# Two-layer conditioned transformer: the order of work at the start of the MLPs and of the layer-1 attention

## The chip, the cores and the metric

The kernel runs on one core of one Trainium2 chip. The metric is the device time of the kernel in microseconds (us); lower is better. The clock of TensorE that the throttle granted was 0.99 of full speed over the profiled execution.

## What is computed

The input x has 128 sequences of 32 tokens with 128 features, and each sequence has a condition vector of 128. Everything is float32. Cut to what matters:

```python
# layer 0: 16 heads of 8
tp = silu(cond) @ Wt + bt                # shift, scale, gate for attention and for the MLP
h = layernorm(x, g1, be1) * (1 + scale_msa) + shift_msa
h = attention(h, Wqkv, bqkv, Wproj, bproj)      # softmax over the 32 tokens of the sequence
x = x + gate_msa * h
h = layernorm(x, g2, be2) * (1 + scale_mlp) + shift_mlp
x = x + gate_mlp * (gelu(h @ W1 + b1) @ W2 + b2)
# layer 1: one head of 128
h = film(rmsnorm(x, norm1_w), cond, film1_w, film1_b)
Q, K, V = h @ q_w + q_b, h @ k_w + k_b, h @ v_w + v_b
x = x + softmax(Q @ K.T / sqrt(128)) @ V @ proj_w + proj_b
h = film(rmsnorm(x, norm2_w), cond, film2_w, film2_b)
x = x + gelu(h @ mlp_w1 + mlp_b1) @ mlp_w2 + mlp_b2
```

## The kernel before, in words

The 4096 tokens are 32 tiles of 128 rows, handled as eight groups (NG = 8) of four tiles. The kernel has four phases: layer-0 attention (phase 0), layer-0 MLP (1), layer-1 attention (2), layer-1 MLP (3). All of x stays in the tile X. A group in a phase has the running number gg = 8 * phase + g, and buffers with two halves are indexed by p = g % 2. Each engine has its own hand-written instruction list, and the order in that list is the order of the work: there is no scheduler. The engines meet through counting semaphores. Each phase is software-pipelined: while group g is multiplied, group gg + 2 is transposed, and the statistics of group gg + 3 are taken.

The path of one group into a phase's matmuls is a chain over four engines, which the steps below speak of as the normalisation chain:

- VectorE (DVE): `row_stats` (L463), `aggregate` (L471 to L483: mv, then sqm, mk, v_sb).
- GpSimd (POOL): `power` (L319 rstd, L321 shift). In phase 2 it is `mean_square` on DVE (L583) and `power1` (L398) instead.
- ScalarE (ACT): `apply` (L750) writes xhat. In phase 2 POOL's `scale_rows` (L391) does.
- TensorE (PE): `rows_T` (L919) transposes xhat into the PSUM bank hT_ps.
- DVE: `modulate` (L492) multiplies it into hA; POOL: `add_shift` (L332) adds the shift, giving h.

In an MLP step PE runs `up(phase, g)` (L943, four chunks of 128x512, into banks 2 to 5), `rows_T(gg + 2)`, then `down(phase, g - 1)` (L1129, 16 matmuls into y_ps, which is bank 1). ACT turns each chunk of `up` into gelu (L805, tile gT, which the trace shows as Kx), then does `apply(gg + 3)`. DVE does `row_stats(gg + 3)`, `modulate(gg + 2)`, `aggregate(gg + 3)` and then `update` (L502 in the phases 0 and 1, L505 in 2 and 3), which empties y_ps. POOL does `add_shift(gg + 2)`, `power(gg + 3)`, and `add_gated` (L355, L357) or `keep` (L348). All these are in this order in each engine's list, so `aggregate(gg + 3)` stands behind `modulate(gg + 2)`, and that waits for `rows_T(gg + 2)`.

Each matmul in float32 is two instructions in the trace, so `up` of two chunks is x4, `down` is x32, and a `rows_T` is x4 (transposes are one each).

The seams between the phases are written out by hand. At the seam from phase 0 to 1 PE ends the attention of group 7 with its second half of `weigh0` (L1014). Then `output_T(7)` (L1028) transposes the attention output On, ACT's `move_o(7)` (L797) copies it, `project0(7)` (L1036) multiplies it by Wproj into bank 1, and DVE's `update(0, 7)` (L502) takes it out of there. `up(1, 0)` has been done inside the attention. What remains there is `up(1, 1)`, in two pairs of chunks, `rows_T(10)` and `rows_T(11)`, and `down(1, 0)`. At the seam from phase 1 to 2, `wait_values1(0)` makes PE wait ahead of `scores1(1)` (L1150) and `values1(0)` (L1163) until POOL has finished `add_gated(1, 7)` (x_updated).

Of the kernel before, what the change touches and what calls it, by code (L numbers as in the profile page):

```python
# [31 lines left out]
NG = NT // TG  # L32
# [26 lines left out]
def build(nc, x, cond, weights, columns, rows, out):  # L59
    with ExitStack() as ctx:  # L60
# [3 lines left out]
        def sem(name):  # L64
            return ctx.enter_context(nc.semaphore(name))
# [54 lines left out]
        stats_done, mv_done, v_ready, rstd_ready = sem("stats_done"), sem("mv_done"), sem("v_ready"), sem("rstd_ready")  # L120
# [4 lines left out]
        xg_ready, y_ready, y_used, x_updated = (  # L125
            sem(n) for n in ("xg_ready", "y_ready", "y_used", "x_updated"))
# [11 lines left out]
        rden_ready, o_used, ot_ready, ot_moved = (sem(n) for n in ("rden_ready", "o_used", "ot_ready", "ot_moved"))  # L138
# [13 lines left out]
        def c(name, i=0):  # L152
            at = C_AT[name][0] + i
            return col[:, at:at + 1]
# [10 lines left out]
        def by_seq(ap):  # L165
            return ap.rearrange("p (b t) -> p b t", t=L)
# [4 lines left out]
        def wait(eng, s, n):  # L171

            if not isinstance(n, int) or n > 0:
                eng.wait_ge(s, n)
# [11 lines left out]
        def known(g, low, high):  # L186

            return not isinstance(g, int) or low <= g < high
# [250 lines left out]
        def _(dve):  # L439
# [46 lines left out]
            def modulate(gg, p, stats_of=None):  # L486

                if stats_of is not None:
                    dve.wait_ge(stats_done, stats_of + 1)
                dve.wait_ge(hT_ready, gg + 1)  # L490
                wait(dve, h_ready, gg - 1)
                dve.tensor_tensor(by_seq(hA[:, p, :]), by_seq(hT_ps[:, :]),  # L492
                                  A[:, seqs(gg)].unsqueeze(2).broadcast_to([P, GB, L]), ALU.mult).then_inc(hA_ready, 1)
# [180 lines left out]
            def mlp(phase):  # L674
                def step(g, p):
                    gg = phase * NG + g
                    skipped = 0 if phase == 1 else NG
                    if isinstance(g, int) and g == 0:
                        if phase == 1:
                            normalise(7, 1, 1)  # L680
                        else:
                            softmax1(7, 1)
                            update(2, 6, 0)
                            normalise1(7, 1)
                    first = isinstance(g, int) and g == 0
                    if phase < 3 or known(g, 0, 5):
                        row_stats(gg + 3)
                    if first and phase == 1:
                        dve.wait_ge(stats_done, gg + 4)
                        aggregate(gg + 3, 1)  # L690
                        update(0, 7, 1)
                        modulate(gg + 2, p)
                    elif phase < 3 or known(g, 0, 5):
                        modulate(gg + 2, p, gg + 3 - skipped)
                        aggregate(gg + 3, 1 - p, False, skipped)
                    elif g < 6:
                        modulate(gg + 2, p)
                    if first and phase == 3:
                        update(2, 7, 1)
                    elif not first:  # L700
                        update(phase, g - 1, 1 - p)
                return step
# [28 lines left out]
        def _(act):  # L731
# [67 lines left out]
            def gelus(m, p, chunks=range(NC)):  # L799

                for n in chunks:
                    if not (isinstance(m, int) and m == 0 and n < 2):
                        act.wait_ge(u_ready, NC * m + n + 1)
                    bias = c("b1_0" if m_layer[0] == 0 else "b1_1", n)
                    act.activation(gT[:, p, n, :], bank[2 + n][:, :], ACT.Gelu, bias=bias).then_inc(g_ready, 1)  # L805
# [45 lines left out]
            def mlp(phase):  # L851
                def step(g, p):
                    m_layer[0] = phase // 2
                    m = (phase // 2) * NG + g
                    first = isinstance(g, int) and g == 0
                    if first and phase == 3:
                        exps1(7, 1)
                    if not (first and phase == 1):
                        gelus(m, p, (0, 1))
                    else:  # L860
                        move_o(7, 1)
                    gelus(m, p, (2, 3))
                    if first and phase == 1:
                        apply(NG + 2, 0)
                    if phase < 3 or not isinstance(g, int) or g < 5:
                        apply(phase * NG + g + 3, 1 - p)
                return step
# [41 lines left out]
        def _(pe):  # L909
# [4 lines left out]
            def rows_T(gg, p):  # L914

                pe.wait_ge(xhat_ready, gg + 1)
                wait(pe, hA_ready, gg)
                for t in range(TG):
                    last = pe.transpose(hT_ps[:, P * t:P * (t + 1)], xhat[:, p, P * t:P * (t + 1)], ident[:, :])  # L919
                last.then_inc(hT_ready, 1)  # L920
# [16 lines left out]
            def up(phase, g, p, chunks=range(NC)):  # L937

                m = (phase // 2) * NG + g
                pe.wait_ge(h_ready, phase * NG + g + 1)  # L940
                for n in chunks:
                    wait(pe, g_ready, NC * (m - 1) + n + 1)
                    last = pe.matmul(bank[2 + n][:, :], w(f"W1_{phase // 2}", n), h[:, p, :], start=True, stop=True)  # L943
                    last.then_inc(u_ready, 3 if isinstance(m, int) and m == 0 and n == 2 else 1)
# [73 lines left out]
            def output_T(g, p):  # L1018

                pe.wait_ge(o_used, 2 * g + 2)  # L1020
                if isinstance(g, int) and g == NG - 1:
                    pe.wait_ge(pt_ready[0], 2 * NG)
                elif isinstance(g, int) and g == NG - 2:
                    pe.wait_ge(g_ready, 2)
                else:
                    pe.wait_ge(k_moved, g + 3)
                for t in range(TG):
                    last = pe.transpose(ot_bank(g)[:, P * t:P * (t + 1)], On[:, p, P * t:P * (t + 1)], ident[:, :])  # L1028
                last.then_inc(ot_ready, 1)
# [88 lines left out]
            def down(phase, g, p, y=(y_ps, y_ps)):  # L1118
                gg, m = phase * NG + g, (phase // 2) * NG + g
                pe.wait_ge(g_ready, NC * (m + 1))  # L1120
                if phase == 1:
                    pe.wait_ge(y_used, gg + 1)
                elif y[0] is y_ps:
                    pe.wait_ge(x_updated, gg + 1)
                for t in range(TG):
                    if y[0] is not y_ps and t == TG // 2:
                        last.then_inc(y_ready, 1)
                    for n in range(NC):
                        last = pe.matmul(y[t // 2][:, P * t:P * (t + 1)], gT[:, p, n, P * t:P * (t + 1)],  # L1129
                                         w(f"W2_{phase // 2}", n), start=(n == 0), stop=(n == NC - 1))  # L1130
                last.then_inc(y_ready, 1)
# [22 lines left out]
            def wait_values1(g):  # L1154
                pe.wait_ge(pt1_ready, g + 1)
                pe.wait_ge(v1_moved, g + 1)
                pe.wait_ge(x_updated, 2 * NG + g + 1)

            def values1(p):
                for t in range(TG):  # L1160
# [6 lines left out]
            def mlp(phase):  # L1167
                def step(g, p):
                    gg = phase * NG + g
                    first = isinstance(g, int) and g == 0  # L1170
                    if first and phase == 1:
                        output_T(7, 1)
                        pe.wait_ge(y_used, NG)
                    elif first:
                        pe.wait_ge(v1_moved, NG)
                        up(phase, g, p)
                    elif not (phase == 1 and isinstance(g, int) and g == 1):
                        up(phase, g, p)
                    if first and phase == 1:
                        up(1, 1, 1, (0, 1))  # L1180
                        project0(7, 1)
                        up(1, 1, 1, (2, 3))
                    if phase < 3 or not isinstance(g, int) or g < 6:
                        rows_T(gg + 2, p)
                    if not first:
                        down(phase, g - 1, 1 - p)
                    elif phase == 3:
                        wait_values1(7)
                        values1(1)
                return step  # L1190
# [64 lines left out]
```

## Time and profile before

| | us |
|---|---|
| median of 3 runs | 274.64 |
| lowest, highest of the 3 | 274.15, 276.51 |
| profiled execution, its own time | 276.22 |
| profiled execution, span of the trace | 274.4 |

| engine | busy us | share of the span |
|---|---|---|
| PE (matmul) | 250.5 | 91% |
| DVE | 163.9 | 60% |
| POOL | 161.4 | 59% |
| ACT | 154.6 | 56% |

Times in the trace are counted from the start of its span. The first matmuls of the layer-0 MLP's steady pattern stand at 121 us, the layer-1 attention goes from about 171 to 211 us, the layer-1 MLP from there to the end. A view with the name "timeline" gives for each piece: start, length, engine, line and operation, tile written and tiles read, and in square brackets the idle time of the engine just ahead of it with what ended that. The "chain that ended last" follows back from the last instruction to what released each step.

### The profile page before, as it was taken

Reading aid. Unit: us, or ns where it says so; the run is one execution under the profiler, and the core shown is the slowest. Engines: PE = TensorE matmul, PEld = TensorE weight load, DVE = VectorE, ACT = ScalarE, POOL = GpSimd, SP = SyncE. Lnnn points to the kernel's source line nnn. Section 1 sums busy time; section 2 is a strip of 40 time slices with the busy share of each in tenths; the row PEclk is TensorE's granted clock in tenths of the full one; section 3 lists DMA queues with packets and bytes.
Section 4 is the critical chain, followed back from the end, with each engine's and each line's share of the span. In section 5 each row is a group of like instructions: output and inputs, shape, how many; then the busy total and the mean of one; then the engine's idle time right before and its main releaser. Section 6 shows DMA issues by size and latency. Waiting matters only on the chain.

```text
span 274.4 us, 9959 instructions
## 1 busy us (share of the span) xinstructions
PE 250.5 (91%) x3772; PEld 188.1 (69%) x3772; DVE 163.9 (60%) x500; ACT 154.6 (56%) x340; POOL 161.4 (59%) x169
## 2 busy tenths in 40 slices
PE   0698887999999997889999999989999999999996
PEld 0556665877878876457777777857676477777775
DVE  4869864769769765354445554488889655441112
ACT  2468645668668675495555455564655655455440
POOL 6544432764864865466676666699999854345110
PEclk9999999999999998999999999999999999999999
DMA  6953332434333451450000000000000001111112
GB/s 223 317 201 85 98 104 77 121 79 125 120 91 110 110 123 40 119 153 4 0 0 0 0 0 0 2 1 5 0 0 0 0 11 32 38 38 39 38 41 76
DMA packets 17450, 18.00 MB, mean 66 GB/s; under 512 B 2320, under 2 KB 13072, under 8 KB 17296
## 3 DMA queue, kind: packets, MB, share of 16 engines
q1 hardware_dynamic: 16848, 15.67, 19.8%
q10 hardware_dynamic: 576, 1.98, 2.1%
q8 instruction: 16, 0.26, 0.4%
q14 instruction: 10, 0.08, 0.1%
HBM read 11.48 MB, written 4.59 MB: 59 GB/s over the span
## 4 chain that ended last, share of the span: by engine, by line
PE 70%; DVE 9%; ACT 7%; issue 7%; POOL 2%; DMA 2%; ACTq 1%; DVEq 0%; SPq 0%; POOLq 0%
PE bank L1129 21%; PE bank L943 17%; PE bank L985 6%; PE bank L998 5%; PE bank L1014 5%; PE bank L919 4%; PE bank L1036 2%; PE bank L950 2%; ACT squares L882 2%; PE bank L958 2%; ACT xhat L750 2%; PE bank L965 2%; DMA X<-x 2%; DVE smax L515 1%; DVE stats L463 1%
## 5 line engine op out<-in xcount | busy, mean ns | idle before, releaser
L750 ACT ACTIVATE xhat<-X,shift,rstd 128x128 f32 (+1 forms) x96 | 40.1, 484 | 47.1 <-POOL shift L321 47.1
L1129 PE MATMUL bank<-W,Kx 128*128 128x128 f32 x512 | 59.6, 275 | 0.0
L1129 PEld LDWEIGHTS bank<-W,Kx 128*128 128x128 f32 x512 | 58.5, 192 | 1.0 <-issue 1.0
L943 PE MATMUL bank<-h,W 128*128 128x512 f32 x124 | 56.8, 599 | 0.2 <-ACT Kx L805 0.2
L332 POOL TENSOR_TENSOR h<-hA,B 128x512 f32<-128x512 f32 x32 | 34.1, 1066 | 27.1 <-DVE hA L492 27.1
L805 ACT ACTIVATE Kx<-bank,col 128x512 f32<-128x512 f32 x64 | 39.1, 676 | 8.6 <-PE bank L943 8.6
L492 DVE TENSOR_TENSOR hA<-bank,A 128x512 f32<-128x512 f32 x32 | 21.9, 686 | 33.1 <-PE bank L919 16.8
L943 PEld LDWEIGHTS bank<-h,W 128*128 128x128 f32 x124 | 22.6, 194 | 22.5 <-issue 22.3
L340 POOL TENSOR_TENSOR Ss<-Sc,smax 128x512 f32<-128x512 f32 x16 | 16.9, 1059 | 35.4 <-DVE smax L515 35.4
L319 POOL TENSOR_TENSOR rstd<-v_sb,minus_half 128x4 f32<-128x4 f32 x24 | 24.6, 1024 | 14.6 <-DVE v_sb L483 9.2
L919 PEld LDWEIGHTS bank<-ident,xhat 128*128 128x128 f32 x128 | 15.9, 146 | 15.6 <-issue 10.5
L355 POOL TENSOR_TENSOR yG<-yG,gate 128x512 f32<-128x512 f32 x16 | 20.3, 1272 | 7.6 <-DVE yG L502 7.6
L348 POOL TENSOR_TENSOR xg<-X,row 128x512 f32<-128x512 f32 x16 | 20.3, 1268 | 7.5 <-DVE X L505 7.4
L919 PE MATMUL bank<-ident,xhat 128*128 128x128 f32 x128 | 20.4, 284 | 3.3 <-ACT xhat L750 2.5
L985 PE MATMUL bank<-Kx,Qs 32*32 32x128 f32 x1024 | 19.1, 272 | 4.2 <-issue 3.5
L505 DVE TENSOR_TENSOR X<-bank,xg 128x512 f32 (+1 forms) x15 | 10.3, 690 | 20.6 <-PE bank L1129 19.8
L463 DVE BATCH_NORM_STATS2 stats<-X 128x6 f32 (+1 forms) x96 | 20.7, 278 | 1.9 <-DMA X<-x 1.9
L357 POOL TENSOR_TENSOR X<-X,yG 128x512 f32 (+1 forms) x16 | 20.3, 1269 | 2.4 <-POOL yG L355 2.1
L783 ACT ACTIVATE Sc<-bank 128x512 f32<-128x512 f32 x16 | 9.5, 596 | 20.8 <-PE bank L985 20.6
L985 PEld LDWEIGHTS bank<-Kx,Qs 32*32 32x32 f32 x1024 | 14.4, 103 | 7.2 <-issue 5.3
L792 ACT ACTIVATE PT<-bank 128x512 f32<-128x512 f32 x32 | 17.4, 595 | 3.1 <-PE bank L998 3.1
L998 PE MATMUL bank<-ident,Ss 128*128 128x128 f32 x128 | 18.5, 289 | 0.1
(117 smaller groups left out, 391.2 us busy)
## 6 DMA issues: line engine op xcount, KB each, us to landing
values_scratch<-Vs SPq DMA_DIRECT2D x8, 288.0 KB, 2.8
Vx<-values_scratch SPq DMA_DIRECT2D x32, 72.0 KB, 2.0
gate<-gates_scratch SPq DMA_DIRECT2D x32, 64.0 KB, 2.2
gate<-gates_scratch SPq DMA_DIRECT2D x16, 128.0 KB, 2.6
out<-X SPq DMA_DIRECT2D x7, 256.0 KB, 2.3
Kx<-Ks SPq DMA_DIRECT2D x24, 64.0 KB, 1.9
W<-weights ACTq DMA_DIRECT2D x1, 1152.0 KB, 6.5
X<-x SPq DMA_DIRECT2D x4, 256.0 KB, 6.7
```

The lines of the kernel that those rows point to most:

```text
L319: pool.tensor_tensor(rstd[:, p, :], v_sb[:, p, :], minus_half[:, :], ALU.pow).then_inc(pool_chain, 1)
L332: pool.tensor_tensor(by_seq(h[:, p, :]), by_seq(hA[:, p, :]), B[:, seqs(gg)].unsqueeze(2).broadcast_to([P, GB, L]), ALU.add).then_inc(h_re ...
L348: pool.tensor_tensor(by_tile(xg[:, p, :]), X[:, x_group(g), :], biases(phase), ALU.add).then_inc(xg_ready, 1)
L463: last = dve.bn_stats(stats[:, t, :], X[:, x_tile(gg, t), :])
L492: dve.tensor_tensor(by_seq(hA[:, p, :]), by_seq(hT_ps[:, :]), A[:, seqs(gg)].unsqueeze(2).broadcast_to([P, GB, L]), ALU.mult).then_inc(hA_ ...
L750: last = act.activation(xhat[:, p, P * t:P * (t + 1)], X[:, x_tile(gg, t), :], ACT.Identity, bias=shift[:, p, t:t + 1], scale=rstd[:, p, t ...
L805: act.activation(gT[:, p, n, :], bank[2 + n][:, :], ACT.Gelu, bias=bias).then_inc(g_ready, 1)
L919: last = pe.transpose(hT_ps[:, P * t:P * (t + 1)], xhat[:, p, P * t:P * (t + 1)], ident[:, :])
L943: last = pe.matmul(bank[2 + n][:, :], w(f"W1_{phase // 2}", n), h[:, p, :], start=True, stop=True)
L985: last = pe.matmul(bank[4 + b % 2][at:at + L, P * slot(b):P * (slot(b) + 1)], Qs[rows_of, p, L * b:L * (b + 1)], Kx[rows_of, p, :, L * b:L ...
L998: last = pe.transpose(bank[1 + 6 * odd][:, at], Ss[:, half, odd, at], ident[:, :])
L1129: last = pe.matmul(y[t // 2][:, P * t:P * (t + 1)], gT[:, p, n, P * t:P * (t + 1)], w(f"W2_{phase // 2}", n), start=(n == 0), stop=(n == N ...
```

## The change

Five edits, all in the order of instructions or in what one wait counts.

1. PE, seam 0 to 1: `up(1, 1)` chunks 0 and 1 go ahead of `output_T(7)`, and chunks 2 and 3 go ahead of `project0(7)`. The wait for `ot_moved` guards bank 3, which `output_T(6)` had used.
2. ACT, seam 0 to 1: the gelus of chunks 2 and 3 of `up(1, 0)` go ahead of `move_o(7)`.
3. PE, step g = 1 of phase 1: `down(1, 0)` goes ahead of `rows_T(11)`.
4. PE, seam 1 to 2: `wait_values1(0)` waits until DVE has read y_ps (`y_used`) in place of waiting until POOL has finished the residual (`x_updated`).
5. DVE, first step of phase 3: `aggregate(27)` goes ahead of `modulate(26)`.

```diff
@@ DVE, mlp step
+                    elif first:
+                        dve.wait_ge(stats_done, gg + 4 - skipped)
+                        aggregate(gg + 3, 1 - p, False, skipped)
+                        modulate(gg + 2, p)
                     elif phase < 3 or known(g, 0, 5):
                         modulate(gg + 2, p, gg + 3 - skipped)
                         aggregate(gg + 3, 1 - p, False, skipped)
@@ ACT, mlp step
                     if not (first and phase == 1):
                         gelus(m, p, (0, 1))
-                    else:
+                    gelus(m, p, (2, 3))
+                    if first and phase == 1:
                         move_o(7, 1)
-                    gelus(m, p, (2, 3))
@@ PE, wait_values1
-                pe.wait_ge(x_updated, 2 * NG + g + 1)
+                if isinstance(g, int) and g == 0:
+                    pe.wait_ge(y_used, 2 * NG + 1)
+                else:
+                    pe.wait_ge(x_updated, 2 * NG + g + 1)
@@ PE, mlp step
                     if first and phase == 1:
+                        pe.wait_ge(ot_moved, NG - 1)
+                        up(1, 1, 1, (0, 1))
                         output_T(7, 1)
-                        pe.wait_ge(y_used, NG)
...
                     if first and phase == 1:
-                        up(1, 1, 1, (0, 1))
+                        up(1, 1, 1, (2, 3))
+                        pe.wait_ge(y_used, NG)
                         project0(7, 1)
-                        up(1, 1, 1, (2, 3))
+                    if phase == 1 and isinstance(g, int) and g == 1:
+                        down(1, 0, 0)
+                        rows_T(gg + 2, p)
+                        return
```

The changed file's line numbers on PE are four higher than before (L943 is L947, L1028 is L1032, and so on). First PE at the start of the layer-0 MLP, before. L1014 is the last `weigh0`, L1028 `output_T(7)`, L943 the chunks of `up(1, 1)`, L1036 `project0(7)`, L919 x8 is `rows_T(10)` and `rows_T(11)`, L1129 is `down(1, 0)`:

```order
L1014 MATMUL bank<-Vx,PT 32x36 x32
L1028 MATMUL bank<-ident,On 128x128 x4
L943 MATMUL bank<-h,W 128x512 x2
L1036 MATMUL bank<-W,OTs 128x128 x4
L943 MATMUL bank<-h,W 128x512 x2
L919 MATMUL bank<-ident,xhat 128x128 x8
L1129 MATMUL bank<-W,Kx 128x128 x16
```

And the same place in the changed kernel:

```order
L1018 MATMUL bank<-Vx,PT 32x36 x32
L947 MATMUL bank<-h,W 128x512 x2
L1032 MATMUL bank<-ident,On 128x128 x4
L947 MATMUL bank<-h,W 128x512 x2
L1040 MATMUL bank<-W,OTs 128x128 x4
L923 MATMUL bank<-ident,xhat 128x128 x4
L1133 MATMUL bank<-W,Kx 128x128 x16
L923 MATMUL bank<-ident,xhat 128x128 x4
```

Both pairs of `up(1, 1)` moved up by one place, and `down(1, 0)` moved ahead of the second `rows_T`.

On DVE at the start of the layer-1 MLP, L492 is `modulate(26)`, L471 to L483 are `aggregate(27)`, L505 is `update(2, 7)`:

```order
 L463 BN_STATS stats<-X 128x6 x4
-L492 TENSOR_TENSOR hA<-bank,A 128x512
-L471 BN_AGGR mv<-stats 128x2 x4
-L479 SCALAR_TENSOR_TENSOR sqm<-mv,kind 128x4
-L481 TENSOR_SCALAR mk<-mv,kind 128x4
-L483 SCALAR_TENSOR_TENSOR v_sb<-sqm,kind,mv 128x4
+L471 BN_AGGR mv<-stats 128x2 x4
+L479 SCALAR_TENSOR_TENSOR sqm<-mv,kind 128x4
+L481 TENSOR_SCALAR mk<-mv,kind 128x4
+L483 SCALAR_TENSOR_TENSOR v_sb<-sqm,kind,mv 128x4
+L492 TENSOR_TENSOR hA<-bank,A 128x512
 L505 TENSOR_TENSOR X<-bank,xg 128x512
```

The seven instructions of `aggregate(27)` now stand ahead of `modulate(26)`; nothing else moved on DVE, and POOL and SP are as before.

## Rows read from the trace of the kernel before

**Rows 1.** The page: busy time, share of the span and instructions of each engine.

```profile
PE 250.5 (91%) x3772; PEld 188.1 (69%) x3772; DVE 163.9 (60%) x500; ACT 154.6 (56%) x340; POOL 161.4 (59%) x169
```

**Rows 2.** Stretches: length, busy PE, PEld, DVE, ACT, POOL, PE's granted clock, DMA.

```profile
112.70:121.20 8.50, 6.49 (x30) 3.83 (x31) 4.58 (x19) 6.88 (x14) 4.43 (x5) 1.00 0.43 126
...
175.70:210.60 34.90, 33.44 (x597) 23.53 (x595) 30.14 (x71) 19.23 (x77) 32.02 (x30) 1.00 0.01 2
```

**Rows 3.** Timeline, 113 to 121 us: start, length, engine, work, [idle before].

```profile
113.60 0.66 PE L1028 MATMUL bank<-ident,On 128*128 128x128 f32 x4 [0.91 <-DVE On L546]
...
114.29 0.60 ACT L797 ACTIVATE OTs<-bank 128x512 f32<-128x512 f32 x1 [3.88 <-PE bank L1028]
...
114.77 0.22 DVE L479 SCALAR_TENSOR_TENSOR sqm<-mv,kind 128x4 f32<-128x4 f32 x1
...
114.91 1.28 ACT L805 ACT_TABLE_LOAD   x1
...
116.90 0.69 DVE L502 TENSOR_TENSOR yG<-bank,row 128x512 f32<-128x512 f32 x1 [1.64 <-PE bank L1036]
...
117.36 3.18 ACT L750 ACTIVATE xhat<-X,shift,rstd 128x128 f32<-128x128 f32 x8
...
120.59 0.66 PE L919 MATMUL bank<-ident,xhat 128*128 128x128 f32 x4 [0.88 <-ACT xhat L750]
```

**Rows 4.** Chain that ended last, one step of the MLP's pattern: start, length.

```profile
128.25 0.44 PE bank L919 x4
128.69 3.57 PE bank L1129 x32
132.26 3.44 PE bank L943 x8
```

**Rows 5.** Timeline of the same step: the normalisation chain behind that rows_T.

```profile
128.90 0.69 DVE L492 TENSOR_TENSOR hA<-bank,A 128x512 f32<-128x512 f32 x1 [2.57 <-issue]
...
132.85 1.65 ACT L750 ACTIVATE xhat<-X,shift,rstd 128x128 f32 x4 [3.25 <-POOL shift L321]
```

**Rows 6.** Busy time by stretch; the column with 1.00 or 0.50 is PE's granted clock.

```profile
41.00:43.00 2.00, 0.20 (x8) 0.00 (x0) 0.31 (x1) 0.00 (x0) 0.26 (x1) 1.00 0.37 137
...
104.00:105.80 1.80, 0.00 (x1) 0.00 (x0) 1.20 (x3) 1.79 (x4) 1.11 (x2) 1.00 0.00 0
...
107.00:108.00 1.00, 1.00 (x8) 1.00 (x7) 0.46 (x2) 0.00 (x0) 0.00 (x0) 0.61 0.46 82
108.00:109.00 1.00, 1.00 (x7) 1.00 (x6) 0.69 (x1) 0.04 (x1) 0.00 (x0) 0.50 0.20 66
109.00:110.00 1.00, 1.00 (x5) 0.91 (x4) 0.00 (x0) 0.74 (x2) 1.00 (x1) 0.50 0.71 180
110.00:111.00 1.00, 1.00 (x3) 0.34 (x2) 0.00 (x0) 0.41 (x1) 0.92 (x2) 0.68 0.73 213
```

**Rows 7.** Timeline of the layer-1 attention, 181 to 192 us.

```profile
181.09 0.46 PE L1150 MATMUL bank<-Ks,Qs 128*32 128x32 f32 x32 [1.35 <-POOL X L357]
...
190.10 1.27 POOL L348 TENSOR_TENSOR xg<-X,row 128x512 f32<-128x512 f32 x1
...
190.66 0.74 DVE L583 TENSOR_SCALAR v_sb<-ssq 128x4 f32<-128x4 f32 x1
...
191.56 1.02 POOL L398 TENSOR_TENSOR rstd<-v_sb,minus_half 128x4 f32<-128x4 f32 x1 [0.18 <-DVE v_sb L583]
```

**Rows 8.** Timeline of the start of the layer-1 MLP, 213 to 221 us.

```profile
213.78 1.26 POOL L348 TENSOR_TENSOR xg<-X,row 128x512 f32<-128x512 f32 x1
...
214.79 0.69 DVE L492 TENSOR_TENSOR hA<-bank,A 128x512 f32<-128x512 f32 x1 [0.78 <-DVE stats L463]
...
215.81 0.82 DVE L479 SCALAR_TENSOR_TENSOR sqm<-mv,kind 128x4 f32<-128x4 f32 x1
...
216.97 1.02 POOL L319 TENSOR_TENSOR rstd<-v_sb,minus_half 128x4 f32<-128x4 f32 x1 [0.36 <-DVE v_sb L483]
...
220.08 0.65 PE L919 MATMUL bank<-ident,xhat 128*128 128x128 f32 x4 [0.74 <-ACT xhat L750]
```

## The prediction

> **What bounds the kernel now.** I read the page first. PE is busy 250.5 us of a span of 274.4 us, the other engines 56 to 60% [rows 1]. So a microsecond counts only where PE stands idle or where PE is made to stand idle. Next come the busy times by stretch: from 112.7 to 121.2 us PE is busy 6.49 us of 8.50, so all that reordering could win there directly is 2.0 us of idle time plus whatever work of PE can be pulled in from behind that stretch [rows 2]. The timeline shows where that idle time lies. PE waits 0.91 us for On ahead of `output_T(7)`, then ACT, which has been idle for 3.88 us ahead of `move_o(7)`, loads a table and does two gelus only afterwards, so that its eight pieces of xhat start at 117.36, and PE waits another 0.88 us for the last of them ahead of `rows_T(11)` [rows 3]. From 121.2 us on PE runs in a pattern without gaps: 0.44 us of rows_T, 3.57 of down, 3.44 of up, 7.45 us for a group [rows 4]. The last two views are those of the other two seams: in the layer-1 attention PE waits 1.35 us once for POOL's residual [rows 7], and at the start of the layer-1 MLP 0.74 us for xhat [rows 8].
>
> **Edits 1 to 3, the seam from attention to MLP.** PE is free 0.91 us ahead of 113.60, at 112.7 [rows 3]. What `up(1, 1)` needs (h of group 9, gelus 0 and 1) is long there, so its first pair runs 112.7 to 114.4: 1.72 us, half of the 3.44 us of a whole up [rows 4]. `output_T(7)` follows, four transposes in 0.44 us [rows 4], its result 0.66 us after its start [rows 3], at 115.1. The second pair needs gelus 2 and 3. ACT was free at 110.4 (114.29 less 3.88 us idle), and load plus two gelus take 2.45 us (114.91 to 117.36) [rows 3], so they are there at 112.9. The second pair runs to 116.6. `move_o(7)` takes 0.60 us [rows 3], to 115.7, long ahead of PE's need. `project0(7)` is 8 instructions of the kind of which down has 32 in 3.57 us [rows 4], so 0.9 us, to 117.5, and `update(0, 7)` on DVE takes 0.69 us [rows 3], to 118.25. ACT starts on xhat of group 10 at 115.7 instead of 117.36 and takes half of 3.18 us [rows 3], so `rows_T(10)` runs at 117.5 to 117.95, and `down(1, 0)` starts behind `update(0, 7)` at 118.3. Before it started at 121.25 (`rows_T(11)` at 120.59 with its result after 0.66 us [rows 3]). So at this point PE is 3.0 us ahead, more than the 2.0 us of idle time, since `rows_T(11)` of 0.44 us is still to come, and PE no longer waits for the end of a result between its parts, save for `update(0, 7)`.
>
> But this head start isn't kept. Edit 3 puts `rows_T(11)` behind `down(1, 0)`: 118.3 + 3.57 = 121.85, which is 1.25 us later than the 120.59 of before [rows 3]. The normalisation chain for group 12 starts at exactly this point, because `aggregate(12)` stands behind `modulate(11)` on DVE, and that waits for `rows_T(11)`. The length of this chain is read in the MLP's pattern: rows_T at 128.25 [rows 4], hA at 128.90, and xhat from 132.85 for 1.65 us, to 134.50 [rows 5]. That is 6.25 us, and with the step to PE 6.3. In the pattern it is hidden, as a period is 7.45 us. Now it isn't: behind `rows_T(11)` PE has only 0.44 + 3.44 us, so it is at `rows_T(12)` at 121.85 + 3.88 = 125.75, while xhat of group 12 is there at 121.85 + 6.3 = 128.15. PE waits 2.4 us. Before, `rows_T(12)` stood at 128.25 [rows 4]. Behind it the list is the same in both and PE is the bound again with 1.1 us of cover. So of 3.0 us gained 0.1 stays: the wait has moved from in front of the pattern into its first step. Bounds: the chain could be 0.3 us quicker or slower here than in the pattern, because POOL is busy with `add_gated` at another time. So edits 1 to 3 bring between -0.4 and +0.2 us, and I take -0.1.
>
> **Edit 4.** PE waits 1.35 us, to 181.09, for POOL's residual [rows 7]. DVE reads y_ps ahead of that residual's first step, so the new wait is over long before, and only `pt1_ready` (PT of group 0, from DVE) is left; I put it at a quarter of the wait, so that `scores1(1)` starts about 1.0 us earlier. That alone moves nothing at the end: in this phase PE is busy 33.44 and POOL 32.02 us of 34.90 [rows 2], so both are close to their bound and each needs the other. What can be won is POOL's idle time. It waits 0.18 us for v_sb, and v_sb (L583) itself takes 0.74 us from 190.66 because it ends only when xg, started at 190.10, is through [rows 7]; six groups with 0.1 to 0.2 us each make 0.8 us, out of the 2.9 us that POOL is idle in the stretch [rows 2]. With PE a microsecond earlier, DVE and ACT can come to L583 about 0.5 us earlier, ahead of xg. The bounds are 0 and -1.2 us (POOL's 0.8 us and PE's own last wait for it); I take -0.7, near what POOL's idle time gives.
>
> **Edit 5.** Before, `modulate(26)` starts at 214.79, sqm of `aggregate(27)` takes 0.82 us under POOL's h, and rstd starts at 216.97 [rows 8]. Free of POOL, sqm takes 0.22 us [rows 3]. In the new order the stats end at 214.0 (214.79 less 0.78 idle [rows 8]), the four aggr take 0.4, and sqm would stand at 214.4, inside POOL's xg, 213.78 to 215.04 [rows 8]. Taking L583 under xg [rows 7] as the measure, it ends when xg does, at 215.05, and mk and v_sb 0.3 us later. Then `modulate(26)` is at 215.35, 0.55 us later than before. POOL's list has `add_shift(26)` ahead of `power(27)`, so rstd can't use the earlier v_sb: before, hA ended at 215.48 and POOL was free of h at 216.61 (216.97 less 0.36), 1.13 us later; now hA ends at 216.05, h at 217.2, and rstd starts there in place of 216.97. So this edit makes PE's wait for xhat, 0.74 us today [rows 8], 0.2 us longer. If sqm slips in ahead of xg instead, modulate keeps its place and rstd starts right behind h, 0.3 us earlier. Bounds -0.3 and +0.7 (the latter where edit 4 has brought `rows_T(26)` forward and the old order would have used it); I take +0.2.
>
> The Trainium skill, "SBUF — State Buffer", section "SBUF: two separate sides", says that VectorE instructions with two SBUF inputs and GpSimd instructions that read SBUF exclude each other for a whole instruction, whichever starts first. By that rule sqm beside xg costs its wait in full and edit 5 is a loss of 0.2 us; without it, it would be nothing. The trace agrees where POOL runs h (0.82 against 0.22 us).
>
> **The sum.** -0.1 - 0.7 + 0.2 = -0.6 us: a span of 273.8 instead of 274.4. The profiled execution took 276.22 us by itself, 0.6% above the median of the runs shown, 274.64; I carry the difference over to the median: 274.0 us.
>
> **The rivals.**
>
> *The new wait costs the clock (slower).* PE was idle from 104.0 to 105.9, and from 107.3 to about 110.6 its granted clock was 0.50, that is 1.2 in place of 2.4 GHz; by the four slices the loss is 0.39 + 0.50 + 0.50 + 0.32 = 1.7 us of PE's work [rows 6]. Around 42 us a wait as long left the clock at 1.00 [rows 6]. So such a wait sometimes costs the clock and sometimes not, which may also be why three runs of before spread from 274.15 to 276.51. The wait that I forecast ahead of `rows_T(12)` is 2.4 us, longer than either, and stands in the bound part of the kernel, so the loss would be paid in full: 274.0 + 1.7 = 275.7 us, slower than before. It decides the result if the wait ahead of `rows_T(12)` is followed by such slices at 0.50, and only there or in a bound stretch like it. Against it: it is one event per run, and the stretch before it is denser than before. The Trainium skill, "TensorE: Matmul & The Clock Gate", section "Part 1: The HAM clock gate", says that half clock is the default and activity releases it, which speaks for this rival.
>
> *The head start is kept.* If the chain behind `rows_T(11)` were short enough (v_sb of group 12 there before PE comes), PE would keep up to 3.0 us, and with edit 4 the time would be 274.64 - 3.0 - 0.5 = 271.1; with half of the wait hidden 272.6. For it: PE is the bound, and 3.0 us of its work really come forward. Against it: `aggregate(12)` cannot start ahead of `modulate(11)`, and the 6.3 us repeat in every group of the pattern.
>
> *Nothing moves.* The layer-1 attention is bound by POOL whatever PE does, L583 stays locked, and edit 5 loses 0.2: 274.64 - 0.1 + 0.2 = 274.7.
>
> **Chances.** Forecast 0.40, clock 0.25, head start kept at least in half 0.15, nothing moves 0.20. A measurement of this kernel can tell about 1% from no change, 2.7 us: faster than that needs nearly the whole head start, 0.10; slower would need two losses of clock, 0.05; within 1% 0.85. The range takes in the clock rival and half of the head start: 272.2 to 276.0.
>
> **What would show it.** Right: PE free of the waits of 0.91 and 0.88 us, `down(1, 0)` at about 118.3, `rows_T(11)` behind it at about 121.9, and a wait of 2 to 2.5 us ahead of `rows_T(12)`, put down to ACT's xhat; a wait ahead of `scores1(1)` of 0.2 to 0.5 us in place of 1.35; sqm in the first step of phase 3 long (0.6 us or more) beside xg. Wrong: `rows_T(12)` at or under 127.5 with the stretch from there unchanged; or a granted clock under 1.00 behind 126 us, which would make the clock rival right; or an L583 that still takes 0.7 us beside xg in each group of the layer-1 attention, which would take away edit 4's share.

## The result, and the profile after

The changed kernel takes 277.06 us (median of 20 runs), the kernel before 274.99 us in as many runs beside it. The ratio is 1.0062, with a 95% interval of 1.0040 to 1.0084: 1.7 us slower. I had forecast 274.0 us with a range of 272.2 to 276.0. Runs in a slower state (one of these 20, at 328.18 us, and a few of those below) are left out of the ratios and of the counts of runs.

The profiled execution took 275.98 us with a span of 274.2 us, and that is no slower than the profiled execution of before. In both the granted clock fell once, at different places. The rest is scatter in the work ahead of the edits: the last weigh0 ends at 110.01 us here and at 112.70 before, and only 1.7 us of that are the fall. In b1 and b2, which have the order of before and no fall between 100 and 112 us, it ends at 111.1; in a4, at full clock throughout, only at 113.2. So two single profiled spans can't be compared to better than a few us, and distances inside them are used below. Here are the page's busy times and the stretches of the changed kernel (length; busy PE, PEld, DVE, ACT, POOL; granted clock; DMA), as in [rows 1] and [rows 2]:

```profile
PE 250.0 (91%) x3772; PEld 187.8 (69%) x3772; DVE 164.3 (60%) x500; ACT 154.5 (56%) x340; POOL 161.3 (59%) x169
...
112.70:121.20 8.50, 8.06 (x55) 6.44 (x54) 2.86 (x10) 5.66 (x13) 4.74 (x5) 1.00 0.34 122
121.20:175.70 54.50, 51.74 (x310) 39.31 (x308) 25.44 (x88) 29.17 (x63) 34.64 (x36) 0.97 0.03 8
```

The work is the same, and the start of the MLP is dense now, 8.06 of 8.50 us. But the stretch behind it, in which PE had no idle time before, is busy for 51.74 of 54.50 us and has a mean granted clock of 0.97. The slices in it show where:

```profile
124.00:126.00 2.00, 0.00 (x0) 0.00 (x0) 0.27 (x2) 1.49 (x4) 1.60 (x3) 1.00 0.00 0
126.00:127.00 1.00, 0.71 (x4) 0.72 (x5) 0.00 (x0) 1.00 (x3) 1.00 (x1) 0.50 0.02 8
127.00:128.00 1.00, 1.00 (x6) 1.00 (x5) 0.39 (x1) 1.00 (x3) 0.14 (x1) 0.50 0.00 0
128.00:129.00 1.00, 1.00 (x7) 1.00 (x6) 0.86 (x6) 0.45 (x1) 0.43 (x1) 0.50 0.06 16
129.00:130.00 1.00, 1.00 (x9) 1.00 (x9) 0.99 (x3) 0.00 (x0) 0.62 (x1) 0.80 0.00 0
```

PE stands idle from 123.5 to 126.3 and then works at 1.2 GHz for 3.1 us; the slices put the whole fall at 3.4 us, its beginning in the wait. The timeline of the changed kernel over the same place (as [rows 3] and [rows 5]; L947 is up, L923 rows_T, L1040 project0, L1133 down):

```profile
109.94 1.98 PE L947 MATMUL bank<-h,W 128*128 128x512 f32 x4
...
115.01 0.69 DVE L502 TENSOR_TENSOR yG<-bank,row 128x512 f32<-128x512 f32 x1 [2.42 <-PE bank L1040]
...
115.85 3.81 PE L1133 MATMUL bank<-W,Kx 128*128 128x128 f32 x32 [0.44 <-DVE yG L502]
...
119.50 0.60 PE L923 MATMUL bank<-ident,xhat 128*128 128x128 f32 x4
119.93 3.60 PE L947 MATMUL bank<-h,W 128*128 128x512 f32 x8
120.41 0.69 DVE L492 TENSOR_TENSOR hA<-bank,A 128x512 f32<-128x512 f32 x1 [3.33 <-PE bank L923]
...
124.51 1.65 ACT L754 ACTIVATE xhat<-X,shift,rstd 128x128 f32 x4 [6.16 <-POOL shift L321]
...
126.29 1.11 PE L923 MATMUL bank<-ident,xhat 128*128 128x128 f32 x4 [2.76 <-ACT xhat L754]
```

`up(1, 1)` starts with no wait behind weigh0, down runs before the second rows_T, and then PE waits 2.76 us for xhat of group 12. To compare executions whose first 110 us differ, I count from the end of the last weigh0 (112.70 before, 110.01 after). The third `rows_T` of the phase, `rows_T(12)`, from where the list is the same in all kernels, stands 15.55 us behind it before and 16.28 us after. The head start is spent and 0.7 us more with it. In the chain that ended last, the clock's part is seen by the length of the pieces:

```profile
126.29 1.11 PE bank L923 x4
127.40 4.58 PE bank L1133 x32
```

c3 is the same kernel once more, and its profiled execution has the same wait of 2.76 us with no fall behind it:

```profile
126.53 0.65 PE bank L923 x4
127.18 3.57 PE bank L1133 x32
```

From the start of `rows_T(12)` to the end of the span it is 147.9 us in the first and 146.4 us in the second, so one fall costs 1.5 us here.

### The profile page after: what moved, and what is told of

Same layout as the page of the kernel before. It is cut to its first block, busy times and chain, and to the rows that moved or that the text cites. A ratio compares the mean times of both kernels' runs of the same rounds, so it can differ in the third digit from the quotient of the medians.

```text
span 274.2 us, 9960 instructions
## 1 busy us (share of the span) xinstructions
PE 250.0 (91%) x3772; PEld 187.8 (69%) x3772; DVE 164.3 (60%) x500; ACT 154.5 (56%) x340; POOL 161.3 (59%) x169
## 4 chain that ended last, share of the span: by engine, by line
PE 67%; DVE 10%; issue 7%; POOL 7%; ACT 4%; DMA 2%; ACTq 1%; POOLq 1%; DVEq 0%; SPq 0%
PE bank L1133 21%; PE bank L947 16%; PE bank L989 6%; PE bank L1002 5%; PE bank L1018 5%; PE bank L923 4%; PE bank L1040 3%; POOL h L332 2%; PE bank L969 2%; PE bank L962 2%; PE bank L954 2%; DMA X<-x 2%; DVE stats L463 2%; POOL rstd L398 1%; DVE smax L515 1%
## 5 line engine op out<-in xcount | busy, mean ns | idle before, releaser
L1133 PE MATMUL bank<-W,Kx 128*128 128x128 f32 x512 | 60.7, 278 | 0.4 <-DVE yG L502 0.4
L1133 PEld LDWEIGHTS bank<-W,Kx 128*128 128x128 f32 x512 | 59.7, 195 | 1.6 <-issue 1.6
L947 PE MATMUL bank<-h,W 128*128 128x512 f32 x124 | 56.3, 595 | 0.0
L492 DVE TENSOR_TENSOR hA<-bank,A 128x512 f32<-128x512 f32 x32 | 21.9, 685 | 34.5 <-PE bank L923 18.6
L947 PEld LDWEIGHTS bank<-h,W 128*128 128x128 f32 x124 | 22.2, 190 | 22.0 <-issue 21.4
L923 PEld LDWEIGHTS bank<-ident,xhat 128*128 128x128 f32 x128 | 15.8, 146 | 17.4 <-issue 14.0
L923 PE MATMUL bank<-ident,xhat 128*128 128x128 f32 x128 | 20.4, 284 | 5.8 <-ACT xhat L754 4.5
L505 DVE TENSOR_TENSOR X<-bank,xg 128x512 f32 (+1 forms) x15 | 10.3, 690 | 20.5 <-PE bank L1133 19.8
L502 DVE TENSOR_TENSOR yG<-bank,row 128x512 f32<-128x512 f32 x16 | 11.1, 692 | 12.0 <-PE bank L1133 9.2
```

## The experiments

Eleven further kernels and the changed kernel once more ran, each beside runs of the kernel before on the same chip. The ratios are to the kernel before. The third column is the distance from the end of weigh0 to `rows_T(12)` in the profiled execution. The fourth counts the runs with a mean granted clock of 0.997 or more, and the fifth is the median span of those runs. One fall of the clock lowers the mean to 0.994, two to 0.988. The row of before takes together the runs beside all twelve; the clocks of the 20 beside the first measurement are not on record.

| kernel | ratio (95%) | to rows_T(12), us | runs at full clock | their span, us |
|---|---|---|---|---|
| before | 1 | 15.55 | 51 of 90 | 272.5 |
| changed | 1.0062 (1.0040 to 1.0084) | 16.28 | 4 of 19 | 273.8 |
| changed again (c3) | 1.0052 (1.0010 to 1.0093) | 16.27 | 2 of 11 | 272.9 |
| a1: without edit 3 | 0.9971 (0.9941 to 1.0000) | 14.07 | 4 of 11 | 271.1 |
| c1: edits 1 and 2 alone | 0.9972 (0.9942 to 1.0002) | 14.07 | 3 of 12 | 271.4 |
| c2: edits 1, 2, 3 | 1.0040 (1.0008 to 1.0071) | 16.27 | 5 of 12 | 273.4 |
| a2: edit 3 alone | 1.0136 (1.0096 to 1.0177) | 17.20 | 0 of 6 | none |
| b1: edit 4 alone | 1.0010 (0.9976 to 1.0044) | 15.54 | 4 of 12 | 272.9 |
| b2: edit 5 alone | 0.9981 (0.9950 to 1.0013) | 15.54 | 7 of 12 | 272.0 |
| a4: changed, wait filled | 1.0039 (1.0008 to 1.0070) | 16.27 | 7 of 12 | 273.8 |
| c4: changed, both waits filled | 1.0039 (1.0009 to 1.0069) | 16.28 | 7 of 12 | 273.8 |
| b3: before, its wait filled | 0.9977 (0.9947 to 1.0007) | 15.54 | 9 of 12 | 272.3 |
| a3: changed, early statistics | 0.9960 (0.9926 to 0.9994) | 13.52 | 7 of 11 | 270.9 |
| b4: a3 with the wait of before filled | 0.9883 (0.9840 to 0.9927) | 13.52 | 6 of 8 | 270.3 |

### Which edit loses: a1, a2, c1, c2

a1 takes edit 3 out of the changed kernel.

```diff
-                    if phase == 1 and isinstance(g, int) and g == 1:
-                        down(1, 0, 0)
-                        rows_T(gg + 2, p)
-                        return
```

> The changed kernel without edit 3 (rows_T(11) ahead of down(1, 0) again). Theory 'chain': the loss is made by edit 3 alone, since it starts the normalisation chain of group 12 behind down(1, 0). Then rows_T(11) stands about 9 us behind the end of weigh0 or less, rows_T(12) follows without a wait 13.6 to 14.2 us behind the end of weigh0 (16.3 in the changed kernel, 15.55 in the kernel before), no clock loss stands there, and the time is 1.5 to 2 us under the kernel before, ratio 0.993 to 0.995. Rival 'other edits' (1 and 2, 4 or 5 lose): ratio stays at 1.004 to 1.008. Rival 'clock only' (the wait costs nothing by itself): rows_T(12) at about the place of the kernel before and ratio 0.999 to 1.001.

The distance and the sign are those of the chain theory: 14.07 us, and no wait ahead of `rows_T(12)`. The ratio, 0.9971, is a smaller gain than expected, and its interval reaches 1.0000. PE in a1, from its timeline:

```profile
117.75 0.63 PE L923 MATMUL bank<-ident,xhat 128*128 128x128 f32 x4 [1.03 <-DVE hA L492]
118.21 3.74 PE L1133 MATMUL bank<-W,Kx 128*128 128x128 f32 x32
...
125.38 0.65 PE L923 MATMUL bank<-ident,xhat 128*128 128x128 f32 x4
```

With weigh0's end at 111.32, PE pays a wait of 1.03 us ahead of `rows_T(11)`, which edit 3 takes away, and nothing later. a2 puts the same four lines into the kernel before and nothing else.

> The kernel before with edit 3 alone. Theory 'chain': down(1, 0) starts at once, rows_T(11) only behind it, so rows_T(12) comes 6.6 us behind rows_T(11), about 17 us behind the end of weigh0 in place of 15.55, with a wait of 2.5 to 2.8 us ahead of it; the time rises by 1.5 us and, where the granted clock falls behind that wait, by 3.2 us: ratio 1.006 to 1.012. Rival 'other edits': no change, ratio 0.999 to 1.001.

It is the worst of all kernels, 1.0136, more than the bound of 1.012, with the wait where the theory has it:

```profile
119.30 3.74 PE L1129 MATMUL bank<-W,Kx 128*128 128x128 f32 x32
122.87 0.60 PE L919 MATMUL bank<-ident,xhat 128*128 128x128 f32 x4
123.31 3.60 PE L943 MATMUL bank<-h,W 128*128 128x512 f32 x8
129.66 0.65 PE L919 MATMUL bank<-ident,xhat 128*128 128x128 f32 x4 [2.75 <-ACT xhat L750]
```

None of its six runs kept the full clock; in the profiled one it fell both at 107 and at 131 us. c1 is the kernel before with edits 1 and 2, c2 with edits 1, 2 and 3.

> The kernel before with edits 1 and 2 alone (no 3, 4, 5). Theory 'chain': these two are the whole gain, rows_T(12) stands 14.1 us behind the end of weigh0 in place of 15.55, and since edits 4 and 5 moved nothing, the time is that of a1: span at a granted clock of 1.00 1.4 us under the kernel before, ratio 0.993 to 0.998. Rival 'edits 4 and 5 gave something back in a1': further under, ratio 0.990 to 0.993.

> The kernel before with edits 1, 2 and 3 (no 4, 5). Theory 'chain': as the changed kernel in all, rows_T(12) 16.3 us behind the end of weigh0 with a wait of 2.7 us ahead of it, the granted clock falling behind it in some runs, ratio 1.004 to 1.008. Rival 'edits 4 and 5 account for the part of the loss that the chain does not explain': ratio 1.001 to 1.004.

c1 equals a1 and c2 has the distance of the changed kernel and, within its interval, its time (at 1.0040 it stands where the bounds of the theory and of the rival meet, and b1 and b2 below have to tell them apart). So the three edits at the first seam carry the result: 1 and 2 win about 0.8 us (both intervals just reach 1), and edit 3 turns that into a loss. With edit 3 the distance is 2.2 us longer, and the ratios of the two pairs, c1 to c2 and a1 to the changed kernel, rise by 1.9 and 2.5 us. Edit 3 starts the normalisation chain of group 12 behind 3.8 us of down.

### Freeing the chain: a3

a3 is the changed kernel, with `aggregate(12)` ahead of `modulate(11)` on DVE, and `power(12)` ahead of `add_shift(11)` on POOL. For this the second step of the phase is written out on both engines (first=2).

```diff
@@ DVE
-                    elif first:
+                    elif first or phase == 1 and isinstance(g, int) and g == 1:
@@ POOL, mlp step
+                    early = phase == 1 and isinstance(g, int) and g == 1
+                    if early:
+                        power(gg + 3, 1 - p)
                     add_shift(gg + 2, p, phase, g)
```

> The changed kernel with aggregate(12) ahead of modulate(11) on DVE and power(12) ahead of add_shift(11) on POOL, so that the chain of group 12 no longer hangs on rows_T(11). Theory 'chain': rows_T(12) comes right behind up(1, 2), 13.5 us behind the end of weigh0 (16.3 in the changed kernel), with no wait and no fall of the clock; the time is 2 us under the kernel before, ratio 0.991 to 0.994. Rival 'clock only': the 0.7 us stay, and only 1.7 us of clock are won: ratio 1.000 to 1.003. Rival 'other edits': no change against the changed kernel, 1.004 to 1.008.

The chain isn't an assumption any more: with rstd of group 12 early, the same `rows_T(11)` behind `down(1, 0)` costs nothing. In a3's timeline rstd stands ahead of h of group 11, and PE goes on without a wait:

```profile
116.11 3.81 PE L1138 MATMUL bank<-W,Kx 128*128 128x128 f32 x32 [0.44 <-DVE yG L507]
...
119.75 0.60 PE L928 MATMUL bank<-ident,xhat 128*128 128x128 f32 x4
119.97 1.02 POOL L319 TENSOR_TENSOR rstd<-v_sb,minus_half 128x4 f32<-128x4 f32 x1 [0.23 <-DVE v_sb L488]
120.19 3.60 PE L952 MATMUL bank<-h,W 128*128 128x512 f32 x8
121.22 1.05 POOL L332 TENSOR_TENSOR h<-hA,B 128x512 f32<-128x512 f32 x1
123.62 0.60 PE L928 MATMUL bank<-ident,xhat 128*128 128x128 f32 x4
```

The distance is 13.52 us, 2.0 less than before and 2.8 less than in the changed kernel. The ratio of 0.9960 is a gain, though a smaller one than the 0.991 to 0.994 that I expected.

### The clock: a4, c4, b3

a4 keeps the long chain and gives PE work in the wait. c4 fills the wait of the kernel before too. b3 fills that one alone, in the kernel before.

```diff
@@ a4, c4: PE, behind rows_T(11)
+                        for _ in range(3):
+                            pe.matmul(bank[6][:, :], ident[:, :], w("W2_0", 0, FF), start=True, stop=True)
@@ b3, c4, b4: PE, attention of group 7, ahead of its first weigh0
+                if last:
+                    pe.wait_ge(g_ready, 1)
+                    for _ in range(2):
+                        pe.matmul(bank[2][:, :], ident[:, :], w("W2_0", 0, FF), start=True, stop=True)
```

> The changed kernel with three matmuls of 128x512 (2.6 us) that nobody reads put between rows_T(11) and up(1, 2), where they fill the later wait. PE then never stands idle there, but the chain is as long. Theory 'the wait costs the clock': rows_T(12) stands where it does in the changed kernel, 16.3 us behind the end of weigh0, but the granted clock stays at 1.00 behind it, and the time is 1.5 us or so under the changed kernel: ratio to the kernel before 1.000 to 1.003. Rival 'the clock does not hang on the wait': the clock falls there as often as in the changed kernel, ratio 1.004 to 1.010.

In a4's profiled execution the wait of 2.76 us has shrunk to 0.18 us and the clock stays at 1.00, while `rows_T(12)` is where the chain puts it, 16.27 us behind weigh0:

```profile
122.65 0.60 PE L923 MATMUL bank<-ident,xhat 128*128 128x128 f32 x4
123.08 2.74 PE L1195 MATMUL bank<-W,ident 128*128 128x512 f32 x6
125.66 3.60 PE L947 MATMUL bank<-h,W 128*128 128x512 f32 x8
129.44 0.65 PE L923 MATMUL bank<-ident,xhat 128*128 128x128 f32 x4 [0.18 <-ACT xhat L754]
```

```profile
128.00:130.00 2.00, 1.82 (x8) 0.76 (x7) 0.00 (x0) 2.00 (x6) 1.82 (x2) 1.00 0.01 4
130.00:132.00 2.00, 2.00 (x20) 2.00 (x20) 1.56 (x6) 1.61 (x3) 1.02 (x2) 1.00 0.03 8
```

> The changed kernel with both waits filled by unread matmuls: 1.7 us ahead of the first weigh0 of group 7, 2.6 us ahead of up(1, 2). Theory 'chain and clock': the granted clock is 1.00 in more than 7 of 10 runs, only the 0.7 us of the chain are left, ratio 0.999 to 1.003, and the span at full clock is that of the changed kernel. Rival 'there is no clock cost': ratio as the changed kernel, 1.004 to 1.008.

> The kernel before with two matmuls of 128x512 (1.7 us) that nobody reads put ahead of the first weigh0 of group 7, where PE waits 1.9 us for ACT's table load and exp. Theory 'the spread of the kernel before is a fall of the clock behind that wait': the mean granted clock is 1.00 in nearly all runs (15 of 28 in the kernel before), and the median falls by 0.5 to 1.2 us, ratio 0.996 to 0.999, with no run in which the clock is at 0.50 around 108 us. Rival 'the clock falls for another reason': as many runs under 1.00 as before, ratio 0.999 to 1.002.

The changed kernel keeps the full clock in 6 of 30 runs (with c3), a4 and c4 together in 14 of 24, the kernel before in 51 of 90. That looks like the price of the unfilled wait. But c2 has the same wait and keeps it in 5 of 12, and three kernels without it keep it as rarely: a1 and c1 in 7 of 23, b1 in 4 of 12. So it isn't shown that the wait of 2.76 us makes full clock rarer, only that a fall can stand behind it. The times agree in direction only: 1.0039 against 1.0062 and 1.0052, with intervals that overlap, and both filled kernels lie above the bounds I had set; c4 also misses the 7 in 10 runs at full clock. c4 is no better than a4, so the second fill shows no gain there, and b3 keeps the full clock in 9 of 12 runs with a ratio whose interval reaches 1.0007. The theory that the spread of the kernel before is the wait at 104 us alone falls as well. In the profiled executions of a1, b2, b4 and c4 the clock fell around 38 us and not at 107, as here in b2, behind a shorter wait:

```profile
37.26 0.40 PE L989 MATMUL bank<-Kx,Qs 32*32 32x128 f32 x3 [1.64 <-issue]
...
39.00:40.00 1.00, 1.00 (x7) 1.00 (x6) 1.00 (x3) 0.74 (x2) 0.21 (x1) 0.50 0.37 55
40.00:41.00 1.00, 1.00 (x7) 1.00 (x6) 1.00 (x5) 0.32 (x1) 1.00 (x2) 0.50 0.07 16
```

None of the fills touches that place.

### Edits 4 and 5 alone: b1, b2

Each is the change's own edit put into the kernel before.

> The kernel before with edit 4 alone (PE waits for y_used ahead of scores1(1)). Theory 'POOL sets the pace of the layer-1 attention': the wait shrinks from 1.35 to 0.3 us, scores1(1) starts a microsecond earlier, and POOL's rstd of group 26 stands as far behind POOL's xhat of group 19 as before, 34.3 us; ratio 0.999 to 1.001. Rival 'the loop takes the head start' (my prediction): 0.7 us nearer, ratio 0.997 to 0.998. Rival 'edit 4 loses' (the changed kernel lost 1.5 us at full clock where the chain explains 0.7): ratio 1.002 to 1.004.

In b1 the wait ahead of `scores1(1)` is 0.35 us (from 1.35), as forecast, and POOL's rstd of group 26 stands 34.29 us behind its xhat of group 19, as before (and as in the changed kernel). Why the head start of PE didn't reach POOL is seen in the first round of b1 (the first line is L583 while POOL stands idle):

```profile
171.93 0.17 DVE L583 TENSOR_SCALAR v_sb<-ssq 128x4 f32<-128x4 f32 x1 [0.69 <-ACT squares L882]
...
178.50 0.46 PE L1150 MATMUL bank<-Ks,Qs 128*32 128x32 f32 x32 [0.35 <-DVE PT L570]
...
181.74 1.04 POOL L391 TENSOR_TENSOR xhat<-X,rstd 128x512 f32<-128x512 f32 x1 [0.24 <-POOL rstd L398]
181.97 0.95 DVE L565 TENSOR_TENSOR St<-St,rden 128x128 f32<-128x128 f32 x1
...
183.79 1.27 POOL L348 TENSOR_TENSOR xg<-X,row 128x512 f32<-128x512 f32 x1
183.87 1.22 DVE L583 TENSOR_SCALAR v_sb<-ssq 128x4 f32<-128x4 f32 x1
```

DVE did come earlier. But its L565, 0.29 us in six of the eight rounds, takes 0.95 us beside POOL's xhat and ends 0.14 us behind it, and so L583 starts 0.08 us behind the start of xg and takes 1.22 us, longer than before. An earlier start that still misses the slot is only a longer wait. In the five rounds behind it L583 takes 0.73 to 0.81 us beside xg, which was one of my signs of being wrong.

> The kernel before with edit 5 alone (aggregate(27) ahead of modulate(26)). Theory 'power(27) stands behind add_shift(26) on POOL, so v_sb is early for nothing': sqm takes 0.6 us beside xg, hA comes 0.45 us later, rstd 0.05 us later, rows_T(27) within 0.1 us of its old distance from up(3, 0), 9.5 us; ratio 0.999 to 1.001. Rival 'edit 5 loses what the chain does not explain': ratio 1.002 to 1.004.

b2 shows the same for edit 5: v_sb is early, and rstd starts when POOL is through with h of group 26.

```profile
212.14 1.27 POOL L348 TENSOR_TENSOR xg<-X,row 128x512 f32<-128x512 f32 x1
...
212.82 0.61 DVE L479 SCALAR_TENSOR_TENSOR sqm<-mv,kind 128x4 f32<-128x4 f32 x1
213.62 0.68 DVE L492 TENSOR_TENSOR hA<-bank,A 128x512 f32<-128x512 f32 x1
...
214.38 1.05 POOL L332 TENSOR_TENSOR h<-hA,B 128x512 f32<-128x512 f32 x1 [0.97 <-DVE hA L492]
215.39 1.02 POOL L319 TENSOR_TENSOR rstd<-v_sb,minus_half 128x4 f32<-128x4 f32 x1
...
218.49 0.65 PE L923 MATMUL bank<-ident,xhat 128*128 128x128 f32 x4 [0.80 <-ACT xhat L754]
```

PE's wait ahead of `rows_T(27)` is 0.80 us, where it was 0.74 [rows 8]. Both ratios have 1 in their interval; that of edit 5, 0.9981, lies just under the bounds, with no sign of a loss.

### The changed kernel again, and the best version: c3, b4

> The changed kernel once more, beside the others of this call on one chip. Ratio 1.004 to 1.008 if the first measurement holds; at full granted clock its span is 0.7 us above the kernel before by the chain, and was 1.5 us above it in four runs. If the 1.5 was scatter, it comes nearer to 0.7 here.

c3 repeats the first measurement, 1.0052. At full clock its two runs have 272.9 us; all six such runs of the changed kernel have a median of 273.2 us, 0.7 above the kernel before. With c2, a4 and c4 it is nearer to 1.1 us, so the 0.7 us of the chain explain most of it, and a few tenths stay open. The same holds where the distance got shorter: at full clock a1 is 1.4 us under the kernel before by a distance 1.5 us shorter, c1 1.1 by 1.5, a3 1.6 by 2.0, b4 2.2 by 2.0. At equal clock the distance accounts for the spans to within 0.6 us, and how often the clock fell goes with most of the rest of the differences in time.

> The changed kernel with aggregate(12) and power(12) early, and with the 1.9 us wait ahead of the first weigh0 of group 7 filled by two unread matmuls. If both theories hold (the chain of group 12, and the clock behind that wait), it has the 1.4 us that a3 won at full clock and loses no clock: median 272.6 to 273.2 us, ratio 0.991 to 0.994. If only the chain holds, it is as a3, ratio 0.996.

b4 takes 272.10 us (median of 8 runs), a ratio of 0.9883, better than the bounds, and beats both kernels. Its chain that ended last has the fill (L1097) where the kernel before waited:

```profile
104.41 0.44 PE bank L1037 x4
104.85 1.72 PE bank L1097 x4
106.70 0.76 PE bank L1023 x53
```

Compared with a3 it has only the fill more, and the two intervals just touch. That the fill is what separates them isn't shown, since b3 alone brought 0.2%, with an interval that holds no gain.

## Why the prediction was wrong

The sum said 0.6 us faster, and the kernel is 1.7 us slower. Three terms failed: that of the first seam was 0.8 us too good, edit 4's was 0.7 us too good, and the clock, for which the sum held nothing, makes about 0.8 us.

**The mechanism at the first seam was right, and its size was off by 0.8 us.** The 0.91 us wait went, down started early, and a wait of 2.76 us stood ahead of `rows_T(12)` for xhat, where I had said 2.4. The term of the sum was -0.1 us and measured +0.7. Three pieces make the difference. Down started 5.84 us behind weigh0 instead of 5.6, as `up(1, 1)`'s first pair took 1.91 us and PE saw `update(0, 7)` 0.15 us late. Down itself took 3.81 us behind a wait, not 3.57. From `rows_T(11)` to `rows_T(12)` it was 6.63 us, not 6.3. I had given this sum a bound of +0.2, with only the chain in it. Each of the other pieces crossed an engine too, and each crossing cost 0.15 to 0.24 us that the back-to-back rows don't show.

**The clock was a rival and should have been in the forecast.** I gave it 0.25 and a price of 1.7 us. The price fits: 0.46 us on rows_T and 1.01 us on down in the changed kernel's profile, 1.5 us. But I had read one fall in the kernel before as a part of both kernels, so that the sum held nothing for the clock, and not asked how often each would have one. The changed kernel falls under full clock in 24 of 30 runs and the kernel before in 39 of 90. The mean granted clocks of these runs, 0.9937 and 0.9968, make 0.8 us of the span. With the 0.7 us of the chain this is 1.5 us, against 1.7 measured. These 0.8 us are an account of the falls and not of their cause: by the counts of a1, c1 and b1 they may come without the new wait, so how much of them the change made stays open. The Trainium skill, "TensorE: Matmul & The Clock Gate", section "Part 1: The HAM clock gate", says that half clock is the default and activity releases it. The 14 of 24 runs with the wait filled agree with that, the 7 of 23 of a1 and c1 do not bear it out.

**Edit 4's term was wrong: 0 for -0.7.** I had chosen the value at which DVE slips in ahead of xg. It came 0.08 us too late for that, since I had left out what POOL does to DVE on the way there (L565, 0.95 us in place of 0.29), though such an instruction beside POOL was in my own rows. The stock that I drew on was too large as well. I had put POOL's wait for v_sb at 0.8 us in six groups; the waits of POOL in the stretch of [rows 2], before, have it twice, 0.4 us in all, and six times POOL's own 0.24 us from rstd to xhat, which no head start of PE shortens:

```profile
POOL xhat L391 <- POOL rstd L398: 1.4, 6, 0.2
POOL rstd L398 <- DVE v_sb L583: 0.4, 2, 0.2
```

"Nothing moves", which I had at 0.20, was right for this edit.

**Edit 5's term, +0.2, measured +0.05.** sqm took 0.61 us beside xg, as said. `modulate(26)` came later as said, but by 0.46 us and not 0.55, and before, rstd had waited 0.36 us for v_sb, which paid for almost all of it.

Had the sum been +0.7 + 0 + 0.05, with the 0.8 us of the clock added, the forecast would have been 1.6 us slower in place of 0.6 us faster; the 0.8 us could not be known before the runs. The range ended at 276.0 because the clock rival was added to the sum that still held edit 4's gain.

## What to carry to other kernels

When a reordering pulls work ahead, follow what is put behind: work that only feeds another engine (here four transposes of 0.44 us together) can be the start of a chain longer than the work left to hide it. Its due time is that chain's length before the next use, or else the wait gained at one place returns one step later, as it did here. Then look at whether the chain's first steps really need the moved instruction: two statements in another order on DVE and POOL were worth more than all five edits. A head start for one engine in a loop that another paces was worth nothing here (b1); look first for a wait of the pacing engine that the head start would shorten.

## What the runs showed of the hardware

The granted clock of PE fell to 0.50 for about 3.4 us behind some single waits and not behind others of the same kind. In the 14 profiled executions PE has 22 waits of 1.6 us or more behind the first 30 us, and a fall follows 8 of them. By place: the wait of 1.6 us at 37 us is followed by a fall in 4 of 6 executions, that of 1.84 to 1.88 us at 104 us in 2 of 11, that of 2.75 or 2.76 us ahead of `rows_T(12)` in 2 of 4, and one of 1.95 us at 43 us by none. No fall stands behind a shorter wait. So the length of a wait alone doesn't decide it, and the runs don't show what does: a1 and c1, which have no such wait behind 107 us, kept the full clock in only 7 of 23 runs.

A VectorE instruction of 128x4 elements took 0.17 us while GpSimd was idle, and 1.22 us when it started 0.08 us behind a GpSimd instruction of 1.27 us on SBUF (b1).
